# Aggregation of a graph layer: VectorE's one-hots and weighted rows for two slots per instruction

## The reference

```
a     = (q[dst] * k[src]).sum(-1) * scale          # per edge and head, 8 heads of 64
e     = exp(a - segment_max(a, dst)[dst])
denom = segment_sum(e, dst)
agg   = segment_sum(e / denom[dst] * v[src], dst)   # (2500, 512)
x     = agg + (x @ Ws + bs) + enc
```

## Time and profile before

| | |
|---|---|
| median of the runs | 3807.46 us |
| profiled execution, span | 3816.9 us |
| profiled execution's own time | 3816.9 us (the span of its one core) |
| PE busy | 2734.7 us (72%), 11106 instructions |
| DVE busy | 2428.3 us (64%), 4726 |
| POOL busy | 1888.1 us (49%), 1813 |
| ACT busy | 1291.4 us (34%), 6512 |
| DMA | 516.91 MB, mean 135 GB/s |

### The profile page before, as it was taken

The page is one execution under the profiler, slowest core; times in us unless marked ns, Lnnn a source line. Parts: engine busy times, 40 slices in busy tenths (PEclk is TensorE's granted clock), DMA queues, the critical chain, the costliest instruction groups (busy, mean ns, idle before and its releaser), DMA issues. The chain is left out here.

```text
span 3816.9 us, 54263 instructions
## 1 busy us (share of the span) xinstructions
PE 2734.7 (72%) x11106; PEld 1830.2 (48%) x11107; DVE 2428.3 (64%) x4726; ACT 1291.4 (34%) x6512; POOL 1888.1 (49%) x1813
## 2 busy tenths in 40 slices
PE   1998666657777749976666577776087898269998
PEld 1785222225455538832222354444075676247776
DVE  6556888876666665578888666666734445775555
ACT  0103888840000010058888100000243221454444
POOL 0113777737777711157777377776400434254444
PEclk8999988969999979989989699999598999679999
DMA  3434666636666653356666366665211322300000
GB/s 120 158 110 135 195 191 195 195 98 185 177 185 176 184 179 118 115 157 192 196 195 194 96 185 178 181 187 165 100 33 61 116 88 98 113 33 34 33 33 32
DMA packets 195443, 516.91 MB, mean 135 GB/s; under 512 B 29816, under 2 KB 30690, under 8 KB 195374
## 3 DMA queue, kind: packets, MB, share of 16 engines
q0 software_dynamic: 107520, 352.41, 32.3%
q1 hardware_dynamic: 76334, 142.71, 11.0%
q10 hardware_dynamic: 11520, 20.98, 1.4%
HBM read 453.19 MB, written 62.79 MB: 135 GB/s over the span
## 5 line engine op out<-in xcount | busy, mean ns | idle before, releaser
L1130 PE MATMUL agg_psA<-agg_wv,agg_hot 128*128 128x264 f32 (+1 forms) x2688 | 757.1, 424 | 274.2 <-DVE agg_hot L1080 181.7
L764 POOL DMA_INDIRECT agg_vbuf<-v_rows,agg_index x672 | 731.8, 1089 | 252.5 <-issue 182.1
L764 POOL DMA_INDIRECT score_kbuf<-k_rows,score_index x672 | 638.0, 949 | 250.6 <-issue 182.1
L1130 PEld LDWEIGHTS agg_psA<-agg_wv,agg_hot 128*128 128x128 f32 x2688 | 510.2, 204 | 521.8 <-issue 457.7
L873 PE MATMUL score_psQ<-layer_q_parts,score_hotT 128*128 x2016 | 555.4, 431 | 214.1 <-ACT score_hotT L903 116.1
L1090 DVE TENSOR_TENSOR agg_wv<-agg_vbuf,agg_wt 128x512 f32<-128x512 f32 x672 | 466.0, 693 | 378.0 <-DMA agg_vbuf<-v_rows,agg_index 375.9
L893 ACT ACTIVATE score_prod<-score_prod 128x64 f32<-128x64 f32 x2688 | 644.1, 241 | 125.9 <-DVE score_prod L837 125.8
L837 DVE TENSOR_TENSOR score_prod<-score_psQ,score_kbuf 128x512 f32<-128x512 f32 x672 | 447.9, 686 | 148.5 <-DMA score_kbuf<-k_rows,score_index 127.1
L893 ACT ACTIVATION_READ_ACCUMULATOR score_prod<-score_prod 128x1 f32 x2688 | 501.9, 187 | 0.0
L102 PE MATMUL proj_psP<-proj_w,proj_xT 128*128 128x512 f32 x1920 | 454.9, 396 | 16.9 <-DVE proj_xT L703 8.9
L873 PEld LDWEIGHTS score_psQ<-layer_q_parts,score_hotT 128*128 128x128 bf16 x2016 | 215.9, 107 | 496.6 <-issue 367.6
(11 more groups left out here) (275 smaller groups left out, 3271.3 us busy)
## 6 DMA issues: line engine op xcount, KB each, us to landing
score_kbuf<-k_rows,score_index POOLq DMA_INDIRECT x672, 3.7
agg_vbuf<-v_rows,agg_index POOLq DMA_INDIRECT x672, 3.8
proj_enc<-xn_rows SPq DMA_DIRECT2D x40, 256.0 KB, 3.0
base_rows<-proj_enc SPq DMA_DIRECT2D x40, 256.0 KB, 2.0
k_rows<-proj_out ACTq DMA_DIRECT2D x40, 256.0 KB, 2.1
v_rows<-proj_out ACTq DMA_DIRECT2D x40, 256.0 KB, 2.1
layer_x<-base_rows SPq DMA_DIRECT2D x40, 256.0 KB, 4.1
xn_rows<-index_x SPq DMA_DIRECT2D x5, 1024.0 KB, 4.3
```

What stands on the lines that cost most here:

```text
L764: pool.indirect_dma_start(bufs[:, u, :], None, table, bass.IndirectOffsetOnAxis(ap=index[:, half, u - half * h:u - half * h + 1], axis=0)) ...
L1130: last = pe.matmul(psA[:, bass.ds(d % 2, 1), e, 0:hi - lo].rearrange("p o w -> p (o w)"), hot[:, u, :], wv[:, u % R, lo:hi], start=False, ...
```

## The change

VectorE's loop in `aggregate` steps over pairs of slots. One comparison with two inputs (`lane` repeated over the pair, `local` repeated over 128 columns) makes two one-hots, 256 columns; one multiply weights two slots, 1024 columns, after waits for both landings. `hots` and `weighted` count pairs, so every wait on them has its value halved; the wait before the one-hots asks for the pair's second slot. `gather` gets a parameter `per`, slots per count of `freed`: 2 from `aggregate`, 1 (as before) from `score_edges`. The copies of weights, TensorE's products, the gathers and their order stay as they are.

```diff
--- before.py
+++ after.py
@@ -751,12 +751,12 @@
                 turns(pool, T2, pair)
 
 
-def gather(pool, T, t, half, bufs, index, table, landed, copied, started, freed, later_):
+def gather(pool, T, t, half, bufs, index, table, landed, copied, started, freed, later_, per=1):
 
     h = U // 2
     if later_:
 
-        pool.wait_ge(freed, (t - 1) * U + half * h + h)
+        pool.wait_ge(freed, (t - 1) * (U // per) + (half * h + h) // per)
     pool.tensor_copy(index[:, half, :], T["src"][:, bass.ds(t * U + half * h, h)]).then_inc(copied, 1)
     pool.wait_ge(copied, t * 2 + half + 1)
     pool.sem_inc(started, 1)
@@ -1044,7 +1044,7 @@
                 def tile(t):
                     if later(t):
 
-                        sp.wait_ge(weighted, t * U)
+                        sp.wait_ge(weighted, t * (U // 2))
                     sp.dma_start(one(x[:, bass.ds(t, 1), :]), base_dram[bass.ds(t * P, P), :]).then_inc(base_in, 16)
                 turns(sp, NT, tile)
                 sp.wait_ge(base_in, 16 * NT)
@@ -1053,7 +1053,7 @@
             def _(pool):
                 def turn(t):
                     for half in range(2):
-                        gather(pool, T, t, half, vbuf, index, v_dram, landed, copied, started, weighted, later(t))
+                        gather(pool, T, t, half, vbuf, index, v_dram, landed, copied, started, weighted, later(t), 2)
                 turns(pool, TURNS, turn)
 
             @block.vector
@@ -1063,7 +1063,7 @@
                 def stage(t, half):
                     if later(t):
 
-                        vec.wait_ge(weighted, (t - 1) * U + half * h + h)
+                        vec.wait_ge(weighted, (t - 1) * (U // 2) + (half * h + h) // 2)
                         vec.wait_ge(beside, (t - 1) * (U // B) + (half * h + h) // B)
                     vec.tensor_scalar(wt[:, half].rearrange("p u h -> p (u h)"),
                                       weights[:, bass.ds((t * U + half * h) * H, h * H)],
@@ -1071,13 +1071,14 @@
                     vec.wait_ge(staged, t * 2 + half + 1)
 
                 def turn(t):
-                    for u in range(U):
+                    for u in range(0, U, 2):
                         if u % h == 0:
                             stage(t, u // h)
                         if later(t):
 
-                            vec.wait_ge(summed, t * U + u + 2 - U)
-                        vec.tensor_scalar(hot[:, u, :], T["lane"][:], local[:, bass.ds(t * U + u, 1)], None,
+                            vec.wait_ge(summed, t * U + u + 3 - U)
+                        vec.tensor_tensor(hot[:, u:u + 2, :], T["lane"][:].unsqueeze(1).to_broadcast([P, 2, P]),
+                                          local[:, bass.ds(t * U + u, 2)].unsqueeze(2).to_broadcast([P, 2, P]),
                                           ALU.is_equal).then_inc(hots, 1)
                         if u % B == 0:
                             if later(t) or u >= R:
@@ -1087,9 +1088,10 @@
                             vec.tensor_scalar(wv[:, u % R:u % R + B, C:AW], wt[:, u // h, u % h:u % h + B, :], 1.0, None,
                                               ALU.mult).then_inc(beside, 1)
                         vec.wait_ge(landed[u], t * 16 + 16)
-                        vec.tensor_tensor(wv[:, u % R, 0:C].rearrange("p (h d) -> p h d", h=H),
-                                          vbuf[:, u, :].rearrange("p (h d) -> p h d", h=H),
-                                          wt[:, u // h, u % h, :].unsqueeze(2).to_broadcast([P, H, D]),
+                        vec.wait_ge(landed[u + 1], t * 16 + 16)
+                        vec.tensor_tensor(wv[:, u % R:u % R + 2, 0:C].rearrange("p u (h d) -> p u h d", h=H),
+                                          vbuf[:, u:u + 2, :].rearrange("p u (h d) -> p u h d", h=H),
+                                          wt[:, u // h, u % h:u % h + 2, :].unsqueeze(3).to_broadcast([P, 2, H, D]),
                                           ALU.mult).then_inc(weighted, 1)
                 turns(vec, TURNS, turn)
 
@@ -1121,9 +1123,9 @@
                         if u % B == 0:
                             tiles = node_tiles(nc, pe, T, t * U + u, B)
                         d = tiles[u % B]
-                        pe.wait_ge(hots, t * U + u + 1)
+                        pe.wait_ge(hots, t * (U // 2) + u // 2 + 1)
                         pe.wait_ge(beside, t * (U // B) + u // B + 1)
-                        pe.wait_ge(weighted, t * U + u + 1)
+                        pe.wait_ge(weighted, t * (U // 2) + u // 2 + 1)
 
                         pe.wait_ge(evicted, d + 1)
                         for e, (lo, hi) in enumerate(parts):
```

## The result

The change made the kernel slower: 3880.0 us median (3872.0 to 3887.3, four runs) against 3807.3 (3805.4 to 3813.8, four runs). The ratio is 1.0189, 95% interval 1.0177 to 1.0201, so +73 us. The profiled execution spans 3870.3 us, 53.4 more than the one before; it is the quickest of the four, 8 us under their median, and that of before lies some 9 us above its median. TensorE's granted clock is 0.89 in both.

A forecast was written before the change was run, and what follows sets the result against it. GpSimd's issuing of 336 gathers per layer was taken to bound the aggregation. Issues +46, index copies +11 and tails +3 gave +60 us on 3807.5, so 3868 us; range 3797 to 3940.

The forecast's parts named there:

- random-phase term: GpSimd's aggregation issues: a blocking stretch d every p, met at a random moment, costs a mean wait of d²/(2p).
- GpSimd's issues bound the stage, through one sensitive point 0.1 us into an issue: Aggregation: lasts as long as issuing 336 gathers, 1.525 us each; an issue stands until a running two-SBUF-input multiply ends.
- Issues, +46: Aggregation gathers: the pair's 1.225 us multiply makes the wait 0.211 us per issue against 0.143, 672 times, +46 us.
- The calibration itself: Gather waits: measured 0.143 us against 0.157 by d²/(2p), a ratio of 0.91 kept for the longer multiply.
- Index copies, +11: Aggregation's 84 index copies: wait grows from 0.284 to 0.420 us each, +11 us (0 to +26).
- The new one-hot, 0 of up to 16: VectorE's paired two-input one-hot, 0.415 us behind the multiply, meets hardly any issue: 0, other end +16 us.
- rival C: GpSimd gets no turn between multiply and one-hot, one stretch of 1.70 us per pair: +189, 3996 us; chance 0.07.
- VectorE's 112 us saved are worth nothing: VectorE's weighting and one-hots fall from 663 to 551 us, all in idle time ended by a landing: 0.
- Tails, +3: End of each layer's aggregation: longer last multiply and one more TensorE slot, 1.7 us, for two layers +3 us.
- Today's one-hot costs GpSimd nothing: Aggregation's one-input one-hot doesn't hold issues, so removing it brings nothing; by the skill page it would give back 17 us.
- Rival A: Aggregation: the phase locks well, only one multiply in eight slots catches an issue, copies never wait: -29, 3779 us; chance 0.14.
- Rival B: Aggregation: the multiply's length doesn't govern the wait, only the tails are left: +3, 3811 us; chance 0.09.

The follow-up runs named there:

- halved multiplies: The kernel before with each weighting multiply cut into two of 256 columns: 3746.8 us, ratio 0.9825.
- pair of 512s: The changed kernel with its 1024-column multiply cut into two of 512 columns behind the same paired waits and counts: 3780.1 us, ratio 0.9927 to the kernel before.

## Why the prediction was right

The forecast was 3868 us by the random-phase term; 3880 was measured, +73 instead of +60. The mechanism held. That the sizes came out so near is in part luck: the issues cost less than forecast and the copies more, and the formula met the wait of the kernel before by two errors that cancel (the third point). Its steps:

- *GpSimd's issues bound the stage, through one sensitive point 0.1 us into an issue.* Right in kind, and now shown from both sides: taking away the second SBUF input at unchanged work takes the wait away (1.089 to 0.950), and lengthening the stretch lengthens it. The place of the point is wrong: a multiply must have begun 0.05 us before the issue, not up to 0.1 us after its start (894.35 and 929.35 above). The longest issue of each kernel says it too: 1.485, 1.999 and 3.067 us for stretches of 0.69, 1.23 and 2.29, the stretch plus 0.79, 0.77 and 0.77.
- *Issues, +46.* 37.6 in the profiled execution. Right within a fifth; 0.91 as the calibration of d²/(2p) was a little high for the longer stretch, (1.145 - 0.946)/0.232 = 0.86, and that with the one-hot's share in it.
- *The calibration itself.* It hides two errors. A multiply of length d can cost an issue d - 0.17 us at most (the longest issues: 0.15 to 0.17 less than the multiply's length over 0.946). With that length the random phase gives, as an estimate, 0.52²/(2 x 1.53) = 0.09 us before and 1.06²/(2 x 3.22) = 0.17 after; behind multiplies 93.3/672 = 0.14 and 115.8/672 = 0.17 were measured. After the change the phase is as good as random: 204 issues held where 672 x 1.06/3.22 = 221 would be. Before, 399 were held where 672 x 0.52/1.53 = 228 would be. So the full length d was too much and the random catch too little, and in the kernel before the two met at 0.91. Had the issues of the kernel before been caught at random, the change would have cost more. Why single multiplies catch more isn't shown.
- *Index copies, +11.* Mis-sized: 19.0. A copy comes at a fixed place, behind the half's eighth issue, and there are only 84 of them; that the phase therefore doesn't average out is a reading, not tested. The other kernels show how far it swings: 735 ns here, 665 with the weighting paired alone, 222 with the still longer multiplies of four slots.
- *The new one-hot, 0 of up to 16.* Its share in the changed kernel is 5.8 us behind 28 issues. The reason given (an issue released by the multiply comes back after the one-hot) holds only while the multiply blocks: with the weights in PSUM 92 issues meet it. The prediction named an issue ending about 0.84 behind a one-hot's end as a sign of rival C; these 28 do so without C, so that sign didn't separate the two.
- *VectorE's 112 us saved are worth nothing.* Right: 109 us less busy, 139 us more waiting for landings.
- *Tails, +3.* Under 1 us in this profile, 3 to 4 with the weights in PSUM.
- *Today's one-hot costs GpSimd nothing.* Right to within some 4 us: with one-input one-hots and PSUM weights the issues take 951 ns. The Trainium skill (SBUF — State Buffer, Who interferes with whom) lets tensor_scalar enter a 2-port mode that contends with GpSimd when its operands fit; this form, with a scalar for each edge from SBUF, shows neither the speed (0.28 us for 128 columns) nor more than 0.07 us of hold. The same section says that an instruction with two SBUF inputs contends with a GpSimd instruction that reads SBUF; every run here agrees on VectorE's side, the size being 0.14 us per gather before and 0.20 after; what GpSimd's instruction reads was not varied.
- *Rival A* (the phase locks well) did not come about for the pairs. The halved multiplies and the pair of 512s look like it: 0.066 and 0.107 us of wait per issue, where the formula alone gives 2 x 0.42²/(2 x 1.42) = 0.124 and 2 x 0.69²/(2 x 2.95) = 0.161, a third to a half of which didn't come. But with the length less 0.17 us it gives 2 x 0.25²/(2 x 1.42) = 0.04 and 2 x 0.52²/(2 x 2.95) = 0.09, less than was measured. So the fixed 0.17 us, which weighs more the shorter the stretch, accounts for the difference from the formula, and no lucky phase is needed for it. No run varied the phase alone.
- *Rival C* (no turn between queued instructions) fell by the issues released after a multiply with the one-hot right behind it (none over 2.0 us), and by the two multiplies of 512.
- *Rival B* fell with every run that changed a length.

One thing stays open. The terms above explain the 53 us between the two profiled executions, while the medians lie 73 apart. Of the other 20 some 8 are what the changed kernel's quickest run, the profiled one, lies under its median, and the rest, 11, is what the profiled execution of the kernel before lies above its own (9 by its span of 3816.9, and a run's time is 2 us more than its span: 3872.0 and 3870.3). What makes one execution of the same kernel longer than another wasn't seen, and so neither was the term that the 20 us belong to.

## What to carry to other kernels

Before merging VectorE instructions to save their fixed cost, look at who else waits for them: beside a stream of gathers issued by GpSimd, a single instruction with two SBUF inputs costs more than in proportion to its length. Per multiply the gathers' waits were 0.03, 0.14, 0.40 and 1.31 us for lengths of 0.42, 0.69, 1.23 and 2.29 us (the two longer ones with their one-hots' share), and here cutting the multiplies in two gained more on GpSimd than it cost on VectorE, which was waiting anyway. If GpSimd's issues are the bound, move the small operand of such a multiply to PSUM first: here that one line gave 3695 us, 3.0% (2.9 to 3.2) under the kernel before and the best of all versions, at the same number of instructions. And read the duration of the same instruction in two stages: 949 against 1089 ns pointed to the whole case.

## What was not expected of the hardware

- In one group of runs, all on one chip, the same kernel took 4172 instead of 3811 us, with register operations of TensorE's sequencer at up to 1397 ns instead of 165. Faster gathers then gained nothing, the run with PSUM weights even lost 3.4%. Whether it is the chip or its state at that time isn't shown; no experiment went after the cause.
- Two queued multiplies of 512 columns took 1.29 us together, though 0.69 each: they overlap by 0.08, and still GpSimd got its turn between them.
- VectorE is hardly held in return: the weighting multiply's longest duration was 767 ns before and 1300 after, at medians of 692 and 1225. So an issue keeps VectorE waiting for at most 0.08 of its own 0.95 us.
